# A decoder layer's last stage with a new order of work on every engine, and loops over batches unrolled

## What is computed

```
x = x + attn(layernorm(x), W_qkv, b_qkv, W_out, b_out)        # 16 heads of 16, over 1024 positions
x = x + cross(layernorm(x), ctx, Wq, Wk, Wv, Wo, biases)      # 16 heads, ctx of 4 x 64 x 256
x = x + ffn(layernorm(x), W_fc, ln_w, ln_b, W_proj)
# ffn: h = x @ ternary(W_fc).T; h = gelu(h); h = layernorm(h) * ln_w + ln_b; h @ ternary(W_proj).T
# ternary(W): sign(W) where |W| is over half its mean magnitude, else 0
```

## Time and profile before

| | us |
|---|---|
| median of 3 runs | 1500.81 |
| the runs | 1500.18 to 1509.94 |
| the profiled execution | 1509.01 |
| its span, first to last instruction | 1507.3 |
| mean granted TensorE clock | 0.90 of 2.4 GHz |

### The profile page before, as it was taken

One profiled execution on the slowest core, in us unless ns is written; L12 is line 12 of the kernel. 1 busy time (PEld: TensorE's weight loads), 2 busy tenths in 40 slices (PEclk: granted clock), 3 DMA queues, 4 the chain that ended last, 5 costly groups with the idle time before them and its releaser, 6 DMA issues.

```text
span 1507.3 us, 20825 instructions
## 1 busy us (share of the span) xinstructions
PE 1290.0 (86%) x6474; PEld 683.8 (45%) x6474; DVE 1074.5 (71%) x2001; ACT 835.1 (55%) x1394; POOL 301.3 (20%) x397
## 2 busy tenths in 40 slices
PE   4878899999999999999999997567778687867866
PEld 3434444444444444444444433234556555655655
DVE  3535769999999985799999976546575756667563
ACT  1211147777777764677777775526446373745632
POOL 3100101100111110110110001333433423343220
PEclk9978759999999995899999999779798898989998
DMA  7898603213333321312340012110010220100000
GB/s 234 263 229 251 162 7 65 44 38 53 65 65 62 65 41 30 60 34 37 65 70 9 6 29 79 43 42 1 0 57 2 54 55 1 56 0 14 15 1 28
DMA packets 64735, 91.73 MB, mean 61 GB/s; under 512 B 10880, under 2 KB 40448, under 8 KB 64640
## 3 DMA queue, kind: packets, MB, share of 16 engines
q1 hardware_dynamic: 48048, 54.74, 13.0%
q0 software_dynamic: 10512, 31.47, 12.1%
q10 hardware_dynamic: 6080, 4.34, 0.9%
HBM read 55.92 MB, written 34.08 MB: 60 GB/s over the span
## 4 chain that ended last, share of the span: by engine, by line
PE 61%; DVE 13%; ACT 8%; issue 8%; POOL 5%; DMA 2%; SPq 2%; ACTq 1%; DVEq 0%; POOLq 0%
PE ps L1230 20%; PE ps L1261 17%; PE ps L1109 10%; PE ps L1250 6%; DVE maxes L793 4%; ACT pe_ L664 4%; DVE xn L769 2%; DVE stats L758 2%; POOL pe_ L500 1%; PE ps L1421 1%; PE ps L1366 1%; ACT prob L609 1%; ACT pT L689 1%; ACT gl L652 1%; PE ps L1341 1%
## 5 line engine op out<-in xcount | busy, mean ns | idle before, releaser
L793 DVE TENSOR_REDUCE maxes<-ps 128x1 f32<-128x512 f32 x1024 | 647.3, 684 | 117.0 <-PE ps L1230 93.9
L609 ACT ACTIVATE prob<-ps 128x1024 f32<-128x1024 f32 x512 | 495.6, 1021 | 208.6 <-PE ps L1250 207.9
L1230 PE MATMUL ps<-Ks,Qs 48*128 48x512 f32 x992 | 409.9, 483 | 9.3 <-issue 2.4
L1230 PEld LDWEIGHTS ps<-Ks,Qs 48*128 48x128 f32 x992 | 168.7, 196 | 327.6 <-DVE maxes L793 285.4
L1250 PE MATMUL ps<-Qs,Ks 50*128 50x512 f32 x1024 | 310.2, 447 | 3.4 <-ACT prob L609 3.4
L1261 PE MATMUL ps<-prob,Vs 128*32 128x512 f32 x2048 | 288.4, 637 | 0.4 <-ACT prob L609 0.3
L1250 PEld LDWEIGHTS ps<-Qs,Ks 50*128 50x128 f32 x1024 | 156.9, 195 | 31.2 <-ACT prob L609 14.8
L301 POOL DMA_DIRECT2D Qs<-qk_scratch x78 | 38.9, 501 | 541.5 <-PE ps L1261 495.5
L664 ACT ACTIVATE pe_<-ps,nmx 128x64 f32<-128x64 f32 x512 | 114.2, 385 | 22.9 <-DVE nmx L965 22.3
L500 POOL TENSOR_TENSOR pe_<-pe_,rsum 128x512 f32<-128x512 f32 x64 | 66.8, 1044 | 208.5 <-DVE rsum L955 208.5
L1421 PE MATMUL ps<-t_p,fT 128*128 128x256 f32 x512 | 90.3, 327 | 18.4 <-DVE fT L1002 18.3
(11 more groups left out here) (110 smaller groups left out, 1321.8 us busy)
## 6 DMA issues: line engine op xcount, KB each, us to landing
qk_scratch<-parts SPq DMA_DIRECT2D x32, 512.0 KB, 5.0
Qs<-qk_scratch POOLq DMA_DIRECT2D x78, 128.0 KB, 4.6
Ks<-qk_scratch POOLq DMA_DIRECT2D x78, 128.0 KB, 7.0
v_scratch<-vx SPq DMA_DIRECT2D x32, 256.0 KB, 4.8
Vs<-v_scratch POOLq DMA_DIRECT2D x13, 512.0 KB, 8.4
xa<-in_x POOLq DMA_DIRECT2D x8, 512.0 KB, 5.7
o_scratch<-ot SPq DMA_DIRECT2D x128, 32.0 KB
on_raw<-o_scratch SPq DMA_DIRECT2D x8, 512.0 KB
```

Of the source, the lines that this page charges most:

```text
L609: act.activation(prob[:, par, h].rearrange("p a q -> p (a q)"), ps[:, 2 * h:2 * h + 2, :].rearrange("p a q -> p (a q)"), ACT.Exp).then_inc ...
L793: dve.tensor_reduce(maxes[:, qc, i // 2, i % 2:i % 2 + 1], ps[:, 3 if early else 5 + max_slot(t) % 3, :], AX.X, ALU.max).then_inc(max_redu ...
L1230: pe.matmul(ps[:, 5 + max_slot(t) % 3, :], stack(Qs[g], j, STACK, slice(q0, q0 + P)), stack(Ks[g], j, STACK, slice(half * 512, (half + 1) ...
```

## The change

**Orders.** Each engine's last stage becomes one straight list for phases c = -2 to 9, each call guarded by `0 <= c < NCH`. In phase c stand: scores 2 to 7 of chunk c and scores 0 and 1 of chunk c+1; out_proj, x1, statistics, normalisation, T2 and the first query tile of chunk c+1 (its second in the next phase); o2 of chunk c; T3 and all of fc, gelu, statistics and apply of chunk c-1; all eight feed-forward tiles of chunk c-2. `f_tile` is split into `f_transpose` and `f_proj`.

**Buffers and semaphores.** `pe_`, `nmx`, `psum`, `rsum` hold a slice for each of the 8 score tiles. The ring's order is a table, RING_PHASE; each kind of operation has a semaphore of its own. `kcur` and `vcur` are gone: TensorE reads `kbd` and `vbd`. `xhat_last` and TAIL are gone. `w_qkv` moves ahead of `w_fc` in SBUF, so `x_b` no longer lies over a weight of the preparation; `x_plus_b(0)` no longer waits for `prep_done`.

**Loops.** The loops over batches and chunks of the middle and last stages are unrolled on all engines; the loops of the first stage stay. Within the middle stage's last group, prepare(0) to prepare(3) stand at units 3 to 6 instead of 4, 6, 8 and 10; prepare(4) comes after out_proj of chunk 0 instead of before.

**SP.** write_out(c-4) stands before the loads of chunk c+1; the reciprocals of the last batch are computed on VectorE after x_recip(1, 7) instead of within chunk 0, and written before load_o(3).

```diff
+RING_PHASE = (("s", 2, 0), ("q2", 1, 0), ("s", 3, 0), ("s", 4, 0), ("s", 5, 0), ("s", 6, 0), ("out", 0, 1), ("out", 1, 1),
+              ("pt", 0, 0), ("pt", 1, 0), ("t3", 0, -1), ("t3", 1, -1), ("s", 7, 0), ("pt", 2, 0), ("pt", 3, 0),
+              ("pt", 4, 0), ("val", 0, 0), ("pt", 5, 0), ("pt", 6, 0), ("t2", 0, 1), ("t2", 1, 1), ("pt", 7, 0),
+              ("q2", 0, 1), ("val", 1, 0), ("s", 0, 1), ("o2", 0, 0), ("o2", 1, 0), ("s", 1, 1))
...
         @block.sync
...
+            for c in range(NCH):
+                if c >= 4:
+                    write_out(c - 4)
+                if c == 2:
+                    sp.wait_ge(recip_done, 2)
+                    r_write(B - 1)
+                    sp.wait_ge(r_written, 16 * B)
+                if c + 1 < NCH:
                     sp.wait_ge(o_normed, c + 1)
+                    load_o((c + 1) // QC, (c + 1) % QC)
                     sp.wait_ge(xb_ready, c + 1)
                     load_xc(c + 1)
...
         @block.gpsimd
...
+            for c in PHASES:
+                rstd_3(c - 1)
+                probabilities(c, 0)
+                x1_plus_b(c)
+                probabilities(c, 1)
+                probabilities(c, 2)
+                x2_plus_b(c - 1)
+                probabilities(c, 3)
+                probabilities(c, 4)
+                rstd_2(c + 1)
+                probabilities(c, 5)
+                probabilities(c, 6)
+                normalise(c + 2)
+                probabilities(c, 7)
                 for blk in range(BLK):
+                    rstd_f(c - 1, blk)
+                x_plus_b(c + 2)
...
         @block.scalar
...
+            for c in PHASES:
+                ft_high(c - 2, 0)
+                ft_high(c - 2, 1)
+                c_exp(c, 1)
+                q2_copy(c, 1)
+                ft_high(c - 2, 2)
+                c_exp(c, 2)
+                ft_high(c - 2, 3)
+                c_exp(c, 3)
+                c_exp(c, 4)
+                ft_high(c - 2, 4)
+                ft_high(c - 2, 5)
+                c_exp(c, 5)
+                c_exp(c, 6)
+                pt_copy(c, 0)
+                pt_copy(c, 1)
+                ft_high(c - 2, 6)
+                ft_high(c - 2, 7)
+                x3_high(c - 1, 0)
+                x3_high(c - 1, 1)
+                pt_copy(c, 2)
+                pt_copy(c, 3)
+                c_exp(c, 7)
+                gelu(c - 1, 0)
+                gelu(c - 1, 1)
+                pt_copy(c, 4)
+                o2_copy(c, 0)
+                pt_copy(c, 5)
+                pt_copy(c, 6)
+                t2_copy(c + 1, 0)
+                t2_copy(c + 1, 1)
+                pt_copy(c, 7)
+                gelu(c - 1, 2)
+                gelu(c - 1, 3)
+                q2_copy(c + 1, 0)
+                o2_copy(c, 1)
+                c_exp(c + 1, 0)
...
         @block.vector
...
+            for c in PHASES:
+                ft_low(c - 2, 1)
+                x_recip(c, 0)
+                x2_stats(c - 1)
+                score_max(c, 3)
+                ft_low(c - 2, 2)
+                x_sums(c, 1)
+                score_max(c, 4)
+                x_sums(c, 2)
+                score_max(c, 5)
+                ft_low(c - 2, 3)
...
+                x2_apply(c - 1)
+                ft_low(c - 2, 4)
+                x_recip(c, 1)
+                score_max(c, 6)
+                ft_low(c - 2, 5)
+                x_recip(c, 2)
+                x_sums(c, 3)
+                x_recip(c, 3)
+                x_sums(c, 4)
+                x_recip(c, 4)
+                for k in range(2):
+                    x1_half(c + 1, k)
+                x1_stats(c + 1)
+                ft_low(c - 2, 6)
+                ft_low(c - 2, 7)
+                x3_low(c - 1)
+                x_sums(c, 5)
+                score_max(c, 7)
+                x_recip(c, 5)
+                x_sums(c, 6)
+                f_out(c - 2)
+                x_recip(c, 6)
+                x1_apply(c + 1)
+                x_sums(c, 7)
+                x_recip(c, 7)
+                if c == 1:
                     reciprocals(1, B - 1, B)
...
+                f_stats(c - 1, 0)
+                f_stats(c - 1, 1)
+                f_apply(c - 1, 0)
+                f_apply(c - 1, 1)
+                f_stats(c - 1, 2)
+                f_stats(c - 1, 3)
+                score_max(c + 1, 0)
+                f_apply(c - 1, 2)
+                x2_half(c, 0)
+                f_apply(c - 1, 3)
+                x2_half(c, 1)
+                score_max(c + 1, 1)
+                x_sums(c + 1, 0)
+                ft_low(c - 1, 0)
+                score_max(c + 1, 2)
...
         @block.tensor
...
-            phase_b(0, False)
-            with pe.Fori(1, B - 1) as b:
-                phase_b(b, False)
-            phase_b(B - 1, True)
+            for b in range(B):
+                phase_b(b, b == B - 1)
...
+            for c in PHASES:
+                f_transpose(c - 2, 0)
+                f_transpose(c - 2, 1)
+                x_scores(c, 2)
+                q2(c, 1)
+                f_transpose(c - 2, 2)
+                f_proj(c - 2, 0)
+                x_scores(c, 3)
+                f_transpose(c - 2, 3)
+                x_scores(c, 4)
+                f_proj(c - 2, 1)
+                x_scores(c, 5)
+                x_scores(c, 6)
+                f_transpose(c - 2, 4)
+                f_proj(c - 2, 2)
+                f_transpose(c - 2, 5)
+                f_proj(c - 2, 3)
+                out_proj(c + 1, 0)
+                out_proj(c + 1, 1)
+                if c == -1:
+                    prepare(4)
+                x_pT(c, 0)
+                f_transpose(c - 2, 6)
+                f_proj(c - 2, 4)
+                x_pT(c, 1)
+                f_proj(c - 2, 5)
+                f_transpose(c - 2, 7)
+                t3(c - 1)
+                x_scores(c, 7)
+                x_pT(c, 2)
+                f_proj(c - 2, 6)
+                x_pT(c, 3)
+                f_proj(c - 2, 7)
+                fc(c - 1, 0)
+                x_pT(c, 4)
+                fc(c - 1, 1)
+                x_values(c, 0)
+                x_pT(c, 5)
+                x_pT(c, 6)
+                fc(c - 1, 2)
+                t2(c + 1)
+                x_pT(c, 7)
+                fc(c - 1, 3)
+                q2(c + 1, 0)
+                x_values(c, 1)
+                x_scores(c + 1, 0)
+                o2(c, 0)
+                o2(c, 1)
+                x_scores(c + 1, 1)
```

More of the change, by code:

```diff
@@ L862, in phase_b @@
                     max_pass(b * NG + g + 1)
-            phase_b(0, False)
-            with dve.Fori(1, B - 1) as b:
-                phase_b(b, False)
-            phase_b(B - 1, True)
+            for b in range(B):
+                phase_b(b, b == B - 1)
             for step in range(3):
@@ L1087, in _ @@
-            phase_c(0, 0)
-            phase_c(1, 1)
-            with dve.Fori(1, B - 1) as b:
-                phase_c(2 * b, 2)
-                phase_c(2 * b + 1, 3)
-            phase_c(NCH - 2, 2)
-            phase_c(NCH - 1, 3, last=True)
-            for blk in range(BLK):
-                for t in TAIL[blk]:
-                    if t > 1:
-                        ft_low(NCH - 2, t)
-                f_stats(NCH - 1, blk)
-                f_apply(NCH - 1, blk, xhat_last)
-            f_out(NCH - 2, 0)
@@ L1302, in phase_b @@
                         values(G, g, U, s)
-                        if end and s % 2 == 0 and 4 <= s < 12:
-                            prepare(s // 2 - 2)
+                        if end and 3 <= s < 7:
+                            prepare(s - 3)
                         if not end:
                             max_tile(G + 1, g1, 4 * s + 3)
-            phase_b(0, False)
-            with pe.Fori(1, B - 1) as b:
-                phase_b(b, False)
-            phase_b(B - 1, True)
+            for b in range(B):
+                phase_b(b, b == B - 1)
             pe.wait_ge(o_copied, 2 * GROUPS)
@@ L1388, in fc, with transposes @@
-            def fc(c, blk, base=4):
-                if blk == 0:
-                    for i in (X_T3, X_T3 + 1):
-                        ready(c, i)
-                    if base:
-                        pe.wait_ge(ft_ready, HT * c)
-                elif blk == 1:
-                    if base:
-                        pe.wait_ge(out_added, 2 * c)
-                else:
+                return n
+            def transposes(r, k, xn):
+                for blk in range(BLK):
+                    n = pe.transpose(ps[:, r, blk * P:(blk + 1) * P], xn[:, blk, k * P:(k + 1) * P], ident[:])
+                return n
@@ L1399, in fc, with t3 @@
+            def t3(c):
+                if not 0 <= c < NCH:
+                    return
+                pe.wait_ge(xn3_ready, c + 1)
+                for k in range(KT):
+                    transposes(x_bank("t3", c, k), k, xn_2).then_inc(t3_done, 1)
+            def fc(c, blk):
+                if not 0 <= c < NCH:
+                    return
```

(6 more changed lines are left out.)

799 lines of the change are left out of this document (354 added, 445 removed).

## The result

The changed kernel takes 1314.93 us as the median of three runs (1306.52 to 1322.93), against 1500.81 before: a ratio of 0.874 with an interval of 0.864 to 0.885. The profiled execution is the one of 1306.52 us; its span of 1304.8 us stands against 1507.3 in the earlier trace rows.

The account below looks back on a forecast made before the run. The prediction took last-stage chunks to be latency-bound by a ring of waits between engines; its last-stage terms ended at 1362 us, less 26 for the middle part's loop edge gave 1336 of span; forecast 1335 us, range 1295 to 1395.

Parts of the forecast that it names:

- a walk through another engine's queue: Full chunk, last stage: VectorE's queue walked in the new order, 41 us without collisions; 48 us with collisions and short waits.

## What to carry to other kernels

When an in-order list is rewritten, first add up every engine's work at full clock (busy time less half of the time at half clock is its least value, not its most): the largest sum is the floor, and a walk through another engine's queue may only be added to where it is above that floor. A price that falls on an engine with waits of its own is paid from them. Idle time on TensorE is to be priced with the clock that goes with it, and a loop edge counts as idle time if nothing hides it. The one-off parts of a new pipeline (here the second chunk) deserve their own walk: 12 us hung on the place of one line.

## What the hardware showed that was not expected

- 2.2 us of idle TensorE, in straight-line code, took the granted clock from 1.00 to 0.50, and it came back only after some 20 us of fully busy TensorE; at loop edges 2.4 and 2.8 us of idle time were followed by 57 and 37 us. The idle times hardly differ, what they cost does: 10.9, 17.9 and 26.2 us. Nor does a longer idle time cost more: behind the 9.77 us in chunk 1 of the changed kernel the clock is back at 1.00 from 990 us on, within 6 us of TensorE's start. And 2.06 us of idle time at the start of its last stage, before 911.97, left the clock at 1.00. What sets how long the clock stays low, and whether it falls at all at some 2 us, no run here tells.
- Taking away a wait can give more than its length: a chunk of the old order lost 8.3 us (7.7 in the mean of five) for 5.1 us of VectorE's time, as the clock rose from 0.87 to 0.97.
- The edge between two passes of a hardware loop costs TensorE 2.4 to 2.8 us of idle time where it is fully busy on both sides, the loop's entry and exit none that the trace lists, and loops in a stage where TensorE waits anyway cost nothing measurable.
